# First attention of an eight-layer network: bf16 parts replaced by fp32 halves, its queries and keys loaded by groups of four heads

## Reference

```python
q = layernorm(x) @ Wq + bq          # scaled by 1/4
k, v = ctx @ Wk + bk, ctx @ Wv + bv
rel = skew(q @ Er.T)                # relative positions, causal part
p = softmax(causal(q @ k.T + rel))
x = x + tanh(g_xattn[0]) * (p @ v)
```

## Time and profile before

| | |
|---|---|
| median of 3 runs | 6405.42 us (6404.94 to 6412.81) |
| the profiled execution | 6402.19 us, span of the profile 6400.5 us |
| busy, share of the span | TensorE 73%, VectorE 62%, ScalarE 44%, GpSimd 31% |
| DMA | 648.40 MB |
| issues in r0 and t0 | rel stored 128 times and loaded 128 times, 640.0 KB each, 5.4 and 6.2 us to landing |

### The profile page before, as it was taken

The page is one execution under the profiler, slowest core; times in us unless marked ns, Lnnn a source line. Parts: engine busy times, 40 slices in busy tenths (PEclk is TensorE's granted clock), DMA queues, the critical chain, the costliest instruction groups (busy, mean ns, idle before and its releaser), DMA issues. The chain is left out here.

```text
span 6400.5 us, 101248 instructions
## 1 busy us (share of the span) xinstructions
PE 4673.8 (73%) x24710; PEld 2852.0 (45%) x24710; DVE 3955.7 (62%) x8261; ACT 2808.6 (44%) x5978; POOL 2015.4 (31%) x3020
## 2 busy tenths in 40 slices
PE   7455666482778972897675767797677887995897
PEld 4113333231453331786233645585555763334533
DVE  6335555547537875444477966558866556885465
ACT  2235554124225752322453556535466323771353
POOL 0114442000007640221353554124542214542242
PEclk9558999796898986998777979999889998996797
DMA  4999885000043320210551232102321115322433
GB/s 158 293 342 196 199 202 157 15 0 0 0 167 103 91 77 4 75 40 27 139 152 61 102 116 72 31 6 83 139 72 42 29 60 169 95 73 85 158 123 102
DMA packets 317804, 648.40 MB, mean 101 GB/s; under 512 B 73170, under 2 KB 128115, under 8 KB 317384
## 3 DMA queue, kind: packets, MB, share of 16 engines
q1 hardware_dynamic: 245912, 450.68, 21.8%
q0 software_dynamic: 71488, 193.32, 12.3%
HBM read 373.99 MB, written 238.70 MB: 96 GB/s over the span
## 5 line engine op out<-in xcount | busy, mean ns | idle before, releaser
L1115 DVE TENSOR_REDUCE t_nmax<-t_aps 128x2 f32<-128x1024 f32 x700 | 838.2, 1221 | 276.2 <-PE t_aps L1037 270.9
L1222 ACT ACTIVATE t_expT<-t_bps 128x512 f32<-128x512 f32 x1290 | 700.9, 599 | 283.8 <-PE t_bps L1056 233.4
L1056 PE MATMUL t_bps<-t_Q,t_K 51*128 51x512 f32 (+2 forms) x1290 | 525.9, 468 | 59.2 <-ACT t_expT L1222 43.4
L1037 PE MATMUL t_aps<-t_K,t_Q 49*128 49x512 f32 (+2 forms) x1400 | 464.6, 460 | 64.7 <-DMA t_K<-k_halves 30.0
L1056 PEld LDWEIGHTS t_bps<-t_Q,t_K 51*128 51x128 f32 (+2 forms) x1290 | 228.4, 189 | 526.2 <-ACT t_expT L1222 372.9
L2474 DVE TENSOR_TENSOR f_hl<-f_h,f_hh 128x512 fp32r<-128x512 f32 x192 | 203.7, 1061 | 411.2 <-ACT f_hh L2399 411.2
L1083 PE MATMUL t_ops<-t_expT,t_V 128*17 128x512 f32 (+1 forms) x2560 | 414.0, 615 | 0.4 <-ACT t_expT L1222 0.4
L3880 ACT ACTIVATE t_relsb<-t_relsb,t_nmax 128x128 f32<-128x128 f32 (+3 forms) x515 | 277.9, 559 | 272.1 <-DVE t_nmax L3853 268.7
L3814 PE MATMUL t_tps<-ident,t_relsb 128*128 128x128 f32 x1280 | 242.8, 292 | 165.5 <-ACT t_expT L3702 154.7
L2763 POOL TENSOR_TENSOR a_crossed<-a_qsb,a_tab 128x256 f32<-128x256 f32 x272 | 268.2, 1007 | 300.2 <-ACT a_qsb L2710 269.8
L1156 POOL DMA_DIRECT2D t_Q<-q_halves x525 | 270.9, 518 | 155.5 <-POOLq L78 86.2
(11 more groups left out here) (431 smaller groups left out, 12509.3 us busy)
## 6 DMA issues: line engine op xcount, KB each, us to landing
rel<-r_out SPq DMA_DIRECT2D x128, 640.0 KB, 5.4
t_relsb<-rel SPq DMA_DIRECT2D x128, 640.0 KB, 6.2
t_Q<-q_halves POOLq DMA_DIRECT2D x420, 64.0 KB, 2.5
t_K<-k_halves POOLq DMA_DIRECT2D x420, 64.0 KB, 2.6
k_halves<-a_parts SPq DMA_DIRECT2D x48, 512.0 KB
q_halves<-a_parts SPq DMA_DIRECT2D x48, 512.0 KB, 5.6
o_xT<-attended SPq DMA_DIRECT2D x32, 512.0 KB, 4.2
f_R<-combine SPq DMA_DIRECT2D x128, 128.0 KB, 2.9
```

The costliest lines, as they stand in the source:

```text
L1037: last = nc.tensor.matmul(aps[:, (t * PPG + i) % 2, x, :], operand(Qr, KA, p, h, slice(t * P, (t + 1) * P)), operand(Kr, KA, p, h, slice(0 ...
L1056: nc.tensor.matmul(bps[:, slot_of(kb, j), :], operand(Kr, KB, p, h, slice(kb * P, (kb + 1) * P)), operand(Qr, KB, p, h, slice(0, S)), star ...
L1115: nc.vector.tensor_reduce(nmax[:, g, t, i * HPT:(i + 1) * HPT], aps[:, (t * PPG + i) % 2], AX.X, ALU.max, negate=True).then_inc(s["maxed"], 1)
L1222: nc.scalar.activation(expT[:, kb % RING, j, :], bps[:, slot_of(kb, j), :], ACT.Exp).then_inc(s["expo"], 1 + (PAD if end else 0))
```

## The change

Three things change, all in the first attention.

a0 is built by `split_qkv`, with the same four jobs and the bias of the values spread over 128 partitions. r0 and t0 read the halves: 48 contraction rows for 96, the operands of the matmuls seen as fp32r; a part's row of 512 columns has 2 KB instead of 1 KB, so the bytes of Q and K per batch stay the same. In r0, three transfers of 512 KB stand for six of 256 KB, Er is split by two operations, and TensorE's loop over heads is written out. In t0, Q and K have one buffer each, filled and freed by groups of four heads: semaphores `in0` to `in3` are one for each group, six transfers of 128 KB fill a group, and they are issued after the mask of the second head of the next group, when the scores of the group have been made. V comes with its ones from DRAM (two buffers, semaphores `vin0` and `vin1`), and `Vg` and its copies are gone.

```diff
 def rel_scores(...):
-    KR = 6 * DH
+    KR = 3 * DH
...
-        erk = sb("erk", [KR, S], BF16)
...
-        Q = sb("Q", [KR, 2, H, S], BF16)
+        erk = sb("erk", [KR, S])
+        halves = sb("halves", [DH, 2, S])
+        Q = sb("Q", [KR, 2, H, S])
...
+        PAIRS = ((0, 0), (0, 1), (1, 0))
...
-                        for i, (qp, kp) in enumerate(TERMS):
+                        for i, (qp, kp) in enumerate(PAIRS):
                             pool.dma_start(Q[i * DH:(i + 1) * DH, p],
-                                           qs[qp - 1].rearrange("(h d) t -> d h t", d=DH)[:, :, ds(b * S, S)]).then_inc(s[f"q{p}"], 16)
+                                           qs[qp].rearrange("(h d) t -> d h t", d=DH)[:, :, ds(b * S, S)]).then_inc(s[f"q{p}"], 16)
...
-                ch.link(nc.vector.tensor_copy(pbf[:, 0, :], er32[0:DH, :]))
-                ch.link(nc.vector.tensor_tensor(r1[0:DH, :], er32[0:DH, :], pbf[:, 0, :], ALU.subtract))
-                ch.link(nc.vector.tensor_copy(pbf[:, 1, :], r1[0:DH, :]))
-                ch.link(nc.vector.tensor_tensor(r1[0:DH, :], r1[0:DH, :], pbf[:, 1, :], ALU.subtract))
-                nc.vector.tensor_copy(pbf[:, 2, :], r1[0:DH, :]).then_inc(s["cast"], 1)
+                ch.link(nc.vector.tensor_copy(fast(halves[:, 0, :]), er32[0:DH, :]))
+                nc.vector.tensor_tensor(fast(halves[:, 1, :]), er32[0:DH, :], halves[:, 0, :], ALU.subtract).then_inc(s["cast"], 1)
...
 def causal_attention(...):
-        Q = sb("Q", [P, 2, H, S], BF16)
-        K = sb("K", [P, 2, H, S], BF16)
-        V = sb("V", [P, 2, NT, H, DH])
-        Vg = sb("Vg", [P, 2, NT, HG, VW])
+        Q = sb("Q", [KR, H, S])
+        K = sb("K", [KR, H, S])
+        V = sb("V", [P, 2, NT, H, VW])
...
+                def load(b, g):
+                    for dst, src, parts in ((Q, qs, (0, 0, 1)), (K, ks, (0, 1, 0))):
+                        for r, part in enumerate(parts):
+                            pool.dma_start(dst[r * DH:(r + 1) * DH, g * HG:(g + 1) * HG, :],
+                                           src[part].rearrange("(h d) t -> d h t", d=DH)[:, g * HG:(g + 1) * HG, ds(b * S, S)]).then_inc(s[f"in{g}"], 16)
...
-                        if h == FROM and more:
-                            wait(pool, "score", b * NU)
-                        if FROM <= h <= FROM + 2 * (KR // DH) and (h - FROM) % 2 == 0 and more:
...
-                            load(1 - p, b + 1, (h - FROM) // 2)
-                        if h == 1:
-                            pool.wait_ge(s[f"in{p}"], it * (16 * NLOAD) + 16 * NLOAD)
+                        if j == 0:
+                            pool.wait_ge(s[f"in{g}"], b * (16 * NLOAD) + 16 * NLOAD)
                             pool.sem_inc(s["loaded"], 1)
...
-                        if j == HG - 1:
-                            wait(pool, "pv", k - 1)
-                            nc.gpsimd.tensor_copy(Vg[:, g % 2, :, :, 0:DH], V[:, p, :, g * HG:(g + 1) * HG, :]).then_inc(s["vh"], 1)
+                        if j == 1 and g == 0 and not first:
+                            wait(pool, "score", b * NU)
+                            load(b, NG - 1)
+                        if j == 1 and g and more:
+                            wait(pool, "score", b * NU + g * GU)
+                            load(b + 1, g - 1)
+                        if j == 2 and g == 2 and more:
+                            wait(pool, "pv", b * NG)
+                            values(1 - p, b + 1)
...
-                    if u.h == 0 and u.t == 0:
-                        wait(pe, "loaded", u.b + 1)
+                    if u.j == 0 and u.t == 0:
+                        wait(pe, "loaded", u.G + 1)
...
 def program(nc, a):
-            qkv(nc, G, "a0", G.X,
-                [("wk", i, "c", "bk", 1.0, ks, i * P) for i in range(KT)] + [("wq", i, "x", "bq", -0.25, qs, i * P) for i in range(KT)],
+            vh = dram("values0", [TOK, 16, 17])
+            split_qkv(nc, G, "a0", G.X,
+                [("wk", i, "c", "bk", 1.0, G.kh, i * P) for i in range(KT)] + [("wq", i, "x", "bq", -0.25, G.qh, i * P) for i in range(KT)],
```

More of the change, by code:

```diff
@@ L1257, in rel_scores, with fast @@
         OFF = [0, P, 3 * P, 6 * P]
+        PAIRS = ((0, 0), (0, 1), (1, 0))
+        def fast(x):
+            return x.bitcast(F32R)
         with nc.Block() as block:
@@ L1296, in _ @@
                         b = it * 2 + p
-                        pe.wait_ge(s[f"q{p}"], it * 96 + 96)
+                        pe.wait_ge(s[f"q{p}"], it * 48 + 48)
                         alone(pe)
[L1299 to L1309, removed]
+                        for h in range(H):
+                            n = b * H + h
+                            pe.wait_ge(s["mm_free_a"], n + 1)
+                            pe.wait_ge(s["mm_free_v"], n + 1)
+                            for t in range(NT):
+                                w = (t + 1) * P
+                                last = nc.tensor.matmul(o[:, h % 2 * NT + t, 0:w], fast(Q[:, p, h, t * P:(t + 1) * P]), fast(erk[:, S - w:S]), start=True, stop=True)
+                            last.then_inc(s["mm"], 1)
                         pe.wait_ge(s["mm"], (b + 1) * H)
@@ L3632, in causal_attention @@
     COL = P // HG
-    KR = 6 * DH
+    KR = 3 * DH
     NU = H * NT
     GU = HG * NT
-    NLOAD = 13
+    NLOAD = 6
     SCORES, EXPO = 4, 3
-    FROM = 3
     WIDTH = [(t + 1) * P for t in range(NT)]
@@ L3642, in causal_attention @@
     EW = (NT - 1) * PITCH + S
-    with phase(nc, name, "in0 in1 loaded rel0 rel1 rel2 rel3 mask masked vones vh score least expo turned cp_dve cp_act pv zero o_free o_st0 o_st1") as (s, sb, ps):
-        Q = sb("Q", [P, 2, H, S], BF16)
-        K = sb("K", [P, 2, H, S], BF16)
-        V = sb("V", [P, 2, NT, H, DH])
-        Vg = sb("Vg", [P, 2, NT, HG, VW])
+    with phase(nc, name, "in0 in1 in2 in3 vin0 vin1 loaded rel0 rel1 rel2 rel3 mask masked score least expo turned cp_dve cp_act pv zero o_free o_st0 o_st1") as (s, sb, ps):
+        Q = sb("Q", [KR, H, S])
+        K = sb("K", [KR, H, S])
+        V = sb("V", [P, 2, NT, H, VW])
         relsb = sb("relsb", [P, HG, sum(WIDTH)])
@@ L3747, in _, with values, batch @@
             def _(pool):
[L3748 to L3756, removed]
+                def load(b, g):
[3 more added lines that the diff above has]
+                                           src[part].rearrange("(h d) t -> d h t", d=DH)[:, g * HG:(g + 1) * HG, ds(b * S, S)]).then_inc(s[f"in{g}"], 16)
+                def values(p, b):
+                    pool.dma_start(V[:, p], vs.rearrange("(t p) h w -> p t (h w)", p=P)[:, ds(b * NT, NT)]).then_inc(s[f"vin{p}"], 16)
+                def batch(it, p, first=False, more=True):
                     b = it * 2 + p
@@ L3780, in batch @@
                         last.then_inc(s["masked"], 1)
-                        if j == HG - 1:
-                            wait(pool, "pv", k - 1)
-                            nc.gpsimd.tensor_copy(Vg[:, g % 2, :, :, 0:DH], V[:, p, :, g * HG:(g + 1) * HG, :]).then_inc(s["vh"], 1)
-                for r in range(KR // DH + 1):
-                    load(0, 0, r)
-                nc.gpsimd.memset(Vg[:, :, :, :, :], 1.0).then_inc(s["vones"], 1)
-                pool.wait_ge(s["vones"], 1)
+                        if j == 1 and g == 0 and not first:
[7 more added lines that the diff above has]
+                            values(1 - p, b + 1)
+                for g in range(NG):
+                    load(0, g)
+                    if g == 0:
+                        values(0, 0)
                 pool.wait_ge(s["mask"], 1)
-                batch(0, 0)
+                batch(0, 0, first=True)
                 batch(0, 1)
@@ L3815, in turn, with values @@
                     last.then_inc(s["turned"], 1)
-                def values(g, par, kb):
+                def values(g, par, kb, p, it, i):
                     if kb == 0:
@@ L3820, in values @@
                         wait(pe, "cp_act", g * 8 + 8)
-                        wait(pe, "vh", g + 1)
+                        wait(pe, f"vin{p}", it * 16 + 16)
                         wait(pe, "zero", 1)
```

26 lines of the change are left out of this document (11 added, 15 removed).

## The result

The change makes the kernel slower: 6561.75 us (6554.69 to 6571.47) against 6405.18 us in the same runs of the kernel before (6390.69 to 6412.81), ratio 1.0256, 95% interval 1.0239 to 1.0272. 6343 was forecast. The profiled execution took 6554.69 us, its span is 6553.0 us.

A forecast was written before the change was run, and what follows sets the result against it. It took VectorE to bound a0, the DMA engines r0, and loads with VectorE's waits for masked tiles to slow t0. Terms −33.0 − 3.0 + 4 − 22 − 8 = −62 took 6405.4 to 6343 us, range 6298 to 6380.

The forecast's parts named there:

- t0, its middle: t0 after its start: parts alternate every 128 KB and overlap better, −8 us, bounds −22 and +10.
- the sentence on TensorE: In t0's middle: one fp32 weight load per head, 190 ns against 105, at most 11 us; taken as 0.
- single buffers stall t0: Rival, 5%: bursts and their issues hold relative rows, every t0 group takes 20.9 us, +82 us; 6433 us in all.
- the 32 that the prediction had named as its limit: Sign of error in t0: VectorE waiting for masks more than 32 us.
- TensorE becomes a bound: Rival, 10%: unhidden fp32 weight loads cost 19 us in r0 and 11 us in t0; 6373 us in all.
- a0: The projections: would take as long as a3, the same function called later, 115.99 us for 148.99; −33.0 us.
- r0, its start: Relative scores up to the first matmul: shorter Er split, three fewer transfers, Q no faster; −3.0 us.
- the prediction's sign of fast rows: In r0: the forecast is wrong if r0 shrinks by 20 us and Q's queue uses under 4 us per MB.
- long rows are fast: Rival, 20%: all fp32 transfers in r0 and t0 move at 3.43 us per MB; 104 us saved, 6301 us in all.
- r0, its middle: Rest of r0: 512 KB parts on sixteen partitions overlap less, stores fill gaps; +4 us, bounds −11 and +29.
- t0, its start: t0 up to its first matmul: waits for six 128 KB transfers, not twelve and V; −22 us, bounds −27 and −12.
- Sum: Whole kernel: the five terms for a0, r0 and t0 together give −62 us, so 6343 us.

The follow-up runs named there:

- b48: The kernel before, with t0's score matmuls contracting over the first 48 of their 96 bf16 rows: 6524.35 us.
- e2_bf16: The changed kernel, with t0's score matmuls reading the upper two bytes of each number as bf16, still 48 rows: 6472.02 us.
- g96bf: g96 with t0's score matmuls reading the upper two bytes of each number as bf16: 6344.51 us.
- g96: The changed kernel with t0's scores over 96 rows (48 to 95 zero, zeroed per group) and r0's Q transfers halved and alternating: 6344.99 us, ratio 0.9925 to before.
- g128: g96 with 128 rows instead of 96 (rows 48 to 127 zero): 6339.73 us.
- sp128: g128 with a group's six Q and K transfers issued in three pairs, behind the second, third and fourth masks: 6339.95 us, ratio 0.9901 to the kernel before.
- e5_r0order: The changed kernel, with each of r0's Q transfers cut into two of 256 KB, alternating rows 0-15 and 16-31: 6566.8 us.
- full48: The changed kernel, with one more bf16 matmul over 128 rows, its result overwritten, ahead of each t0 score matmul: 6445.39 us.
- the four g runs: The changed kernel with 64, 80, 96 or 128 zero-padded score rows in t0 and r0's Q order repaired: 6535.57, 6361.58, 6344.99 and 6339.73 us.

## Why the prediction was wrong

**The failed step is t0, its middle**, and in it the sentence on TensorE, which priced the edit by one weight load of 85 ns more a head, 11 us, and took 0. It had t0 at −8; it measured +215.8. The step assumed that 48 rows with the same columns are the same work for TensorE at the same clock. The sum of the earlier trace rows had t0 at clock 0.91 with TensorE busy for 394 us; I read the busy share as slack and did not ask what kept the clock up. One more line of arithmetic on the same row would have put a price on it: 394 us of matmuls at the upper level are up to 789 at the lower one, more than the 583 us that t0 took, and TensorE was in fact busy for 765. b48 gives the part of the clock, +118. The comparison of e2_bf16 with after gives nearly all of the rest: 93 us for fp32 operands, which are hidden at the high clock but for 10 us at most (g96bf) and exposed at the low one. The two do not add up as separate costs: the second exists because of the first.

The weight load was mis-sized as well. 85 ns hold at the high clock (198 ns for 100, g96 and g96bf), where taking 0 was right within 10 us. At the low clock the loads take 270 ns for 98, and there are 512 of them in t0 and not 128. The reason for the 0, that a load runs beside the matmul before it, does not hold there; the kernel after,

```profile
702.08 0.28 PEld L3806 LDWEIGHTS t_sps<-t_K,t_Q 48*128 48x128 f32 x1 [0.33 <-issue]
702.09 0.47 PE L3806 MATMUL t_sps<-t_K,t_Q 48*128 48x128 f32 x1
```

and the two other score matmuls between 700 and 704 us show the same: the load starts within 0.01 us of its own matmul, and at most 0.07 us before the records of the matmuls ahead of it end. The ends of matmuls in a profile are modelled, so this is an indication and no proof.

That the rest of the step was sound is shown by the runs with the clock up: 588.3 (g96) and 578.8 us (g128) for before's 583.5, +5 and −5 where I had −8. GpSimd's lost copies, the bursts and the issues are worth next to nothing together (the bursts by themselves: sp128). The rival *single buffers stall t0* had the right side and a wrong mechanism: VectorE waits for masks three times, 23.3 us for the 32 that the prediction had named as its limit. *TensorE becomes a bound* had the mechanism, but looked for it in r0 and gave t0 11 us; it happened in t0 only.

**a0**, forecast −33.0: −34.2. To price a phase by another call of its function held within 1.2 us.

**r0, its start**, −3.0: −2.8. Rows of 2 KB are not faster while Q is alone: in the kernel after, 148 to 158 us,

```profile
q0 software_dynamic: 293, 1.07, 103.1%
```

107 GB/s, where the earlier trace rows gave 111 for rows of 1 KB. Mixed with the stores, 18.8% of 240 us for 9.44 MB are 4.78 us per MB, where the prediction's sign of fast rows was under 4. That refutes *long rows are fast*, as argued. By the Trainium skill ("SBUF — State Buffer", "Door 1: The DMA port swizzle") sixteen partitions reach 4 of 16 ports, about 109 GB/s; the trace agrees. By the same section rows 0 to 15 and 16 to 31 reach different ports, which is what e5_r0order alternates; the 11.7 us agree with it, but no run tells ports from the mere size of a transfer.

**r0, its middle**, +4: +11.9, right in kind ("two neighbouring parts overlap less") and mis-sized; the present row was the wrong end to lean on. e5_r0order takes 11.7 us off r0.

**t0, its start**, −22: −24.5. The first matmul came 15.9 us behind the first issue.

**Sum.** The first four terms measure −34.2 − 2.8 + 11.9 − 24.5 = −49.6, where I had −54. The kernel with the clock and the order of Q repaired ends 48 us (g96), 53 us (g128) and 58 us (sp128) below the kernel before; the forecast was 62. By the table the spans differ by +152.5 where −62 was forecast, 214.5 us off: t0's middle measured 223.8 above its term and r0's middle 7.9 above, the other three terms came 3.5 lower together, and the phases that were not edited 13.7 lower. Nearly all of the error is the clock with what it exposed.

Of the clock, the Trainium skill ("TensorE: Matmul & The Clock Gate", "Part 1: The HAM clock gate (the "warmup" mystery)") says that it follows how busy TensorE has lately been. In t0 after, TensorE is busy for 765 of 799 us at 0.55; full48 is busy for 622 of 678 at 0.89. By busy time alone the first should have the higher clock, so the measurement decides: what the matmuls fill counts too. Rows alone do not decide either: in r0 of the kernel before the matmuls fill 96 rows, TensorE is busy for 160.91 of 293 us, and the clock is 0.50. The same page's "Part 4: PE-mode transpose" says that transposes do not count as busy in the same way. t0 after would fit, at 0.55 though nearly half of its matmuls' time is full 128-row transposes; no run here took them away.

**Open:** why 49 and 51 rows suffice in the later attention. Its score matmuls have 512 columns each where t0's have 320 in the mean, they follow each other faster (847 in 310 us, for 516 in 799), its products with V have 512 columns each too, and it has no 128-row transposes; none of these was varied alone. Open as well is what lifts the clock for moments in t0 after, as from 585 to 598 us.

## What to carry to other kernels

A contraction that is halved saves TensorE nothing in columns and can cost it its clock. When a change lowers the rows of matmuls, ask what else in the stretch fills the array, and what the stretch would take at half clock; if that exceeds the present bound, pad with zero rows (free here in DMA, 17 us of memsets on an idle VectorE in g96, 4 of them ahead of the first load) before anything else. Price operands at the clock they will have, and by whether TensorE is the bound: fp32 instead of bf16 cost 190 ns a matmul and 93 us at the low clock, 92 ns and at most 10 us at the high one.

## What the runs showed of the hardware

- Rows of zeros count: 48 rows 0.55, 64 rows 0.57, 80 rows 0.85, 96 rows 0.94, 128 rows 0.96, all fp32r with the same columns (after and the four g runs).
- A kernel can be made faster by work for nothing, which raises the clock: 6445.4 us for 6561.8 (49 and 157 us above the kernel before beside each), t0 121.5 us shorter (full48).
- An fp32r score matmul takes 412 ns, a bf16 one of the same shape 320 ns at the high clock (g96, g96bf); 599 and 409 ns at the low one (after, e2_bf16). The difference hardly depends on the columns: 185 ns at 128 and 193 ns at 512.
- The weight load of an fp32 score matmul takes 198 ns at the high clock and 270 ns at the low one, that of a bf16 one 100 and 98 ns (96 rows in g96 and g96bf, 48 in after and e2_bf16).
- The change, with 128 rows, r0's transfers in order and t0's in pairs (sp128), is worth having: 6339.95 us, 1% below the kernel before and 3.4% below the change as made.
